# Loading the first weight chunk of a conditional adapter as two half transfers from two queues

## What is computed

```
dWd = ((h @ Wdd.T + bdd) * 0.1).reshape(B, 128, 512)     # Wdd: 65536 x 128
dWu = ((h @ Wdu.T + bdu) * 0.1).reshape(B, 512, 128)     # Wdu: 65536 x 128
down = relu(einsum('bld,bnd->bln', x, Wd + dWd) + bd)    # x: 4 x 1024 x 512
out  = x + einsum('bln,bdn->bld', down, Wu + dWu) + bu
```

## Time and profile before

| | |
|---|---|
| median of 3 runs | 212.09 us (211.4 to 212.16) |
| the profiled execution, its own time | 211.89 us |
| its span, first to last instruction | 210.1 us |
| TensorE matmul busy | 169.7 us, 81% |
| VectorE busy | 159.9 us, 76% |
| GpSimd busy | 74.1 us, 35% |
| ScalarE busy | 57.6 us, 27% |
| bytes moved | 85.11 MB, mean 405 GB/s |

### The profile page before, as it was taken

How to read it: one execution, slowest core, us unless ns; L and a number is a source line. 1 busy time by engine, 2 the same in 40 slices (tenths; PEclk the granted TensorE clock), 3 DMA queues, 4 the chain that set the end, 5 groups by cost and what they waited for, 6 DMA issues and landing times.

```text
span 210.1 us, 3048 instructions
## 1 busy us (share of the span) xinstructions
PE 169.7 (81%) x1148; PEld 100.7 (48%) x1148; DVE 159.9 (76%) x88; ACT 57.6 (27%) x103; POOL 74.1 (35%) x58
## 2 busy tenths in 40 slices
PE   1066597755699384999987999999999999998980
PEld 0011151322174031476752867678666756557960
DVE  2868997999999999854764958459769999982770
ACT  2000023202011202043550554454453534543000
POOL 2000000000000000035952857599587487897000
PEclk9999996999559969699996999999999999999997
DMA  6999999999999999999999999999999999999997
GB/s 223 425 412 421 424 423 420 420 424 423 421 416 424 423 423 420 423 426 418 421 421 421 416 418 423 418 424 420 424 420 423 423 420 420 415 384 384 315 338 249
DMA packets 19368, 85.11 MB, mean 405 GB/s; under 512 B 1430, under 2 KB 9627, under 8 KB 10140
## 3 DMA queue, kind: packets, MB, share of 16 engines
q1 hardware_dynamic: 19344, 84.94, 99.5%
q10 hardware_dynamic: 12, 0.00, 0.0%
HBM read 76.55 MB, written 8.39 MB: 404 GB/s over the span
## 4 chain that ended last, share of the span: by engine, by line
PE 44%; DMA 41%; DVE 11%; issue 1%; SPq 0%; DVEq 0%
DMA w<-in_L_cond_Wdd_dram 30%; PE bank L649 14%; PE acc L531 12%; DVE wt L300 11%; DMA w<-in_L_cond_Wdu_dram 11%; PE dn L625 10%; PE bank L614 5%; PE gt L557 1%; PE acc L659 1%; SPq L228 0%; DVE xs L342 0%; DVEq L341 0%
## 5 line engine op out<-in xcount | busy, mean ns | idle before, releaser
L300 DVE STREAM_TRANSPOSE wt<-w 128x2048 f32<-128x2048 f32 x63 | 145.5, 2311 | 35.1 <-DMA w<-in_L_cond_Wdu_dram 25.2
L531 PE MATMUL acc<-wt,st 128*32 128x512 f32 x496 | 73.2, 719 | 31.1 <-DVE wt L300 31.1
L481 POOL TENSOR_TENSOR xs<-xs,bu_all 128x1024 f32<-128x1024 f32 x16 | 37.9, 2368 | 108.9 <-PE bank L614 108.9
L531 PEld LDWEIGHTS acc<-wt,st 128*32 128x32 f32 x496 | 14.7, 123 | 68.7 <-issue 37.7
L649 PE MATMUL bank<-wu_b,down 128*128 128x128 f32 (+1 forms) x192 | 30.9, 313 | 0.5 <-issue 0.5
L625 PE MATMUL dn<-xt,wd_b 128*128 128x256 f32 x128 | 30.5, 381 | 0.0
L649 PEld LDWEIGHTS bank<-wu_b,down 128*128 128x128 f32 x192 | 26.5, 191 | 6.6 <-issue 4.5
L488 POOL TENSOR_TENSOR xs<-up_s,xs 128x512 f32<-128x512 f32 x20 | 25.2, 1281 | 4.4 <-ACT up_s L434 4.4
L625 PEld LDWEIGHTS dn<-xt,wd_b 128*128 128x128 f32 x128 | 23.0, 190 | 3.5 <-issue 0.8
L417 ACT ACTIVATE xt<-bank 128x512 f32<-128x512 f32 x32 | 17.4, 595 | 13.2 <-PE bank L614 13.2
L375 ACT ACTIVATE g_rows<-acc 128x512 f32<-128x512 f32 x16 | 9.6, 598 | 39.8 <-PE acc L531 38.5
(11 more groups left out here) (35 smaller groups left out, 36.2 us busy)
## 6 DMA issues: line engine op xcount, KB each, us to landing
w<-in_L_cond_Wdd_dram SPq DMA_DIRECT2D x32, 1024.0 KB, 7.4
w<-in_L_cond_Wdu_dram SPq DMA_DIRECT2D x32, 1024.0 KB, 10.1
xs<-in_x_dram SPq DMA_DIRECT2D x8, 1024.0 KB, 12.3
out_dram<-xs SPq DMA_DIRECT2D x4, 1024.0 KB, 10.8
out_dram<-xs SPq DMA_DIRECT2D x7, 512.0 KB, 5.6
out_dram<-xs SPq DMA_DIRECT2D x2, 256.0 KB, 4.9
base_d<-in_L_cond_Wd_dram SPq DMA_DIRECT2D x1, 256.0 KB, 7.2
down<-in_L_cond_bdd_dram SPq DMA_DIRECT2D x1, 256.0 KB, 7.4
```

The source lines that it names most:

```text
L300: nc.vector.transpose(wt[:, tslot].rearrange("p r (k j) -> p k r j", j=QUAD), w[:, slot, :].rearrange("p (k r h) -> p k r h", r=R, h=QUAD) ...
L481: nc.gpsimd.tensor_tensor(xs[:, b, i0:i0 + UNIT_I], xs[:, b, i0:i0 + UNIT_I], bu_pair, ALU.add).then_inc(bu_added, 1)
L531: last = nc.tensor.matmul(a[TILE * place:TILE * (place + 1)], st[:, r, low * TILE:(low + 1) * TILE], wt[:, slot + h, r], start=low == 0 an ...
```

## The change

The load of the first chunk of Wdd is divided by partitions. SP issues partitions 0 to 63 in the place where it issued all 128. ScalarE issues partitions 64 to 127 as its very first instruction, ahead of its three small loads, on a new semaphore `first_loaded`. VectorE waits for that semaphore ahead of its first transposition, and then for the slot's own semaphore as before. All other chunks are loaded as before.

```
+        first_loaded = sem("first_loaded")
...
             def load_chunk(c, chunk, slot):
                 if later(c, W_RING):
                     sp.wait_ge(wt_ready, c - W_RING + 1)
-                sp.dma_start(w[:, slot, :], chunk).then_inc(w_loaded[slot], 16)
+                rows = slice(0, P // 2) if isinstance(c, int) and c == 0 else slice(0, P)
+                sp.dma_start(w[rows, slot, :], chunk[rows]).then_inc(w_loaded[slot], 16)
...
+            dve.wait_ge(first_loaded, 16)
             turn(0)
             with dve.Fori(1, TURNS) as it:
                 turn(it)
...
         @block.scalar
         def _(act):
+            act.dma_start(w[P // 2:P, 0, :], wdd_chunks[0, P // 2:P]).then_inc(first_loaded, 16)
             act.dma_start(cond_rows, cond.rearrange("b (r i) -> b r i", i=QUAD)).then_inc(cond_loaded, 16)
```

## The result

The changed kernel takes 214.14 us (median of 6 runs, 213.45 to 214.65) against 211.88 us of the kernel before (6 runs). The ratio is 1.0114, with a 95% interval from 1.0095 to 1.0133. It is 2.3 us slower, where 212.0 us and no difference were forecast, and it lies above the range, which ended at 213.0.

A forecast was written before the change was run, and what follows sets the result against it. Loads were taken to bound the kernel to about 110 us, then TensorE with loads close behind. Stream -0.1 us, condition load 0 and added wait 0 took the median from 212.09 to 212.0 us; range 211.2 to 213.0 us.

The forecast's parts named there:

- The first chunk's own transfer: Start of the load stream: between 1.04 us gained and 1.39 us lost by loading in two halves; 0.1 us gain taken.
- the second half starting only after the first: Rival at chunk 0's load: the second half pays a start of its own, 1.39 us, giving 213.5 us; chance 4%.
- Three loads behind half a chunk: ScalarE's queue at the start: condition vectors come with the first chunk, about 5.7 us, not 2.13; far end 8.26 us.
- Where the delay of VectorE goes: First transpositions: VectorE starts 2.1 us later but catches up by chunk 4 with 0.5 us to spare, costing 0.
- The cover of the stream: Chunk 4's issue moves from 8.02 to 10.1 us; up to 14.5 us is early enough, a cover of 4.4 us.
- The signs: Expected in the trace: DMA share full from about 3 us, no hole near 16 us, chunk 4 at 18.2 to 18.4 us.
- The chances: Whole kernel: 83% within 0.5% of the time before, 6% faster by more, 11% slower.

The follow-up runs named there:

- e9: Kernel before, with eight mid-second-stage chunks (t = 8 to 15 of Wdu) each loaded as two transfers, partitions 0 to 63 and 64 to 127: 240.73 us, ratio 1.134.
- e11: Kernel before, with eight mid-second-stage chunks each loaded as two transfers, the even and then the odd partitions: 211.95 us, ratio 1.0005.
- e13: Changed kernel, with even partitions of chunk 0 from SP and odd ones from ScalarE in place of lower and upper half: 212.02 us, ratio 1.0016.
- e3: Changed kernel, with chunk 0 divided by columns over the two queues, all 128 partitions in each transfer: 211.51 us, ratio 1.0002.
- e4: Kernel before, with all of chunk 0 issued by ScalarE in front of its condition load: 213.26 us, ratio 1.0104.
- e8: Kernel before, with all of chunk 0 issued by ScalarE behind its condition load: 211.92 us, ratio 1.0006.
- e14: Changed kernel, with chunk 0 divided into even and odd partitions and ScalarE's condition load in front of its transfer: 212.21 us, ratio 1.0032.
- e10: Kernel before, with eight mid-second-stage chunks each loaded as two transfers by column halves, all 128 partitions: 212.06 us, ratio 1.0021.
- e15: Changed kernel, with chunk 0 divided by columns over both queues and ScalarE's condition load in front of its transfer: 212.56 us, ratio 1.0041.
- e7: Kernel before, with the first four chunks each loaded by SP as two transfers by column halves: 213.18 us, ratio 1.0058.
- e2: Changed kernel, with both partition halves of chunk 0 issued by SP, one behind the other: 213.77 us, ratio 1.0094.
- e6: Kernel before, with the first four chunks each loaded by SP as two transfers, partitions 0 to 63 and 64 to 127: 221.03 us, ratio 1.0438.
- e5: Kernel before, with chunk 0 loaded by SP in three transfers, partitions 0 to 31, 32 to 95 and 96 to 127: 213.66 us, ratio 1.0086.

## Why the prediction was wrong

**The step that failed** is the rate, in "The first chunk's own transfer". It said: "The bytes are the same and pass the same DMA engines", and bounded the loss by one more start of a transfer, 1.39 us. That the rate itself could depend on the partitions of a transfer was in neither bound nor in a rival. No row of before has a transfer of fewer than 128 partitions with many bytes, so 420 GB/s was carried over to a shape for which nothing had shown it. The term measured -2.2 us of stream (0.91 MB at 420 GB/s, and 2.23 us at chunk 4) where +0.1 was taken.

The Trainium skill has a rule that the prediction did not use (SBUF — State Buffer, section Door 1: The DMA port swizzle): the partitions 0 to 63 reach 8 of the 16 ports through which DMA writes, those from 64 on the other 8, and bit 6 of the partition number decides. By that rule each half goes at half the rate. The 242 and 200 GB/s of the change and the 224 of e9 agree with it. The ports themselves are in no trace. The same page of the Trainium skill remarks (section "Can I just issue two DMAs to hit both halves?") that only one transfer spanning all 128 partitions reaches all ports. Read as 128 partitions written, that is not borne out: in e11 transfers of 64 partitions, every second one, ran at 420 GB/s. The rule that the prediction did quote, "Don't bother — they serialize", was read as a price of nothing. Two transfers at half the rate one after the other are slower than the one that they replace.

**The rival that came nearest**, the second half starting only after the first, had 4% and 213.5 us. The order came true: SP's queue moved nothing before 4 us. Its price, a second start of 1.39 us, did not: in e13 the halves follow each other in the same way at no such cost, and what cost the change 2.2 us was the rate within each half.

**Three loads behind half a chunk**: right where the rate is full. The forecast was about 5.7 us for the condition vectors; e3 measured 5.88 and e13 5.62. In the change ScalarE's own half landed at about 5.7 us (4.9 us after its issue at 0.76), but the vectors came at 8.11, with SP's half (7.3 us after 0.75). "With the first chunk" held in all three; the first chunk was late.

**Where the delay of VectorE goes**: right. In e3 and e13 a start over 2 us late was made up by chunk 4, at 18.45 and 18.56 us (18.41 before). In the change the idle time in front of chunk 4 was 0.80 us, about that of before.

**The cover of the stream**: its size was wrong. It let an issue of chunk 4 be early enough up to 14.5 us, from the 1.39 us latency of a load with hardly a byte. In e4 an issue at 12.93 us was already too late. By the first chunk's own rows a large load needs 2.43 us from its issue until its bytes are in full flow, which would have put the limit at 13.5 us for chunk 4; even that is above 12.93. e8 shows that 11.54 us is early enough. Where between the two the limit lies, and what sets it, stays open.

**The signs**: a DMA share that is full from 3 us on was to show that all is well. It was full in the change, with 0.91 MB missing; the GB/s beside it had the loss.

**The chances**: slower had 11%. The range held the ends of the terms it knew, and the missing term was larger than all of them.

## What to carry to other kernels

Do not cut a transfer at partition 64 to spread it over queues or to start it earlier. Even and odd partitions cost nothing that can be told in e11, 0.2% in e13 and 0.3% in e14; columns cost nothing in e3, 0.2% in e10, 0.4% in e15 and 0.6% in e7. No cut gained anything here. Where one transfer's rate is the time of the kernel, a new shape of transfer is a new price, and a row for another shape does not bound it. When GB/s fall while the DMA share stays near 1, look at what the transfers reach before looking at queues and waits.

## What the runs showed of the hardware

Loads into one side of partition 64 moved 200 to 254 GB/s (203 in e2, 207 to 227 in e6, 224 in e9, 200 to 254 in the change) with the engines at a share near 1, where full loads moved 420; the partitions 0, 2, 4 ... and 1, 3, 5 ... as transfers of 64 moved 420. A packet of 8 KiB took 0.54 us in such a half and 0.31 us in a full load. Full loads queued among such halves were in part slowed with them: 11.2 MB at 224 GB/s in e9, of which at most 8.4 MB were halves, and in e5 the first 0.39 MB of chunk 1, in by 8 us, with 177 GB/s from 5.68 us on; a stretch of 352 GB/s in e6 shows that it is not so for all. ScalarE's small load, issued behind half a chunk or a whole one on its queue, came in with chunk 0: 5.62 us in e13, 5.88 in e3, 8.11 in the change, and 8.47 in e4, where chunk 0 and SP's chunk 1 ran side by side.
